# The two arrays of a triangular solver laid transposed in memory, and its GpSimd loops run the other way round

## The chip, the cores and the metric

One core of a Trainium2 chip runs the whole kernel in one launch. The metric is device time in microseconds (us); the kernel before was run three times, and the median is compared. Five engines work side by side: TensorE (PE in the profile; its weight loads stand as PEld), VectorE (DVE), ScalarE (ACT), GpSimd (POOL) and SyncE (SP, which here only issues DMAs). They tell each other of finished work through semaphores.

## The reference

The kernel computes one block of a network on x of shape (2, 4096, 512), all in float32. After a layer norm two branches read the same normed rows and are both added to x:

```python
x = L0_attn_x
xn = _layernorm(x, axis=-1)
x = x + _L0_attn_ref(xn, ...) + _L0_ffn_ref(xn, ...)
```

The attention branch is a gated delta rule: projections to q, k (16 heads of 16) and v (16 heads of 32), a causal convolution of four taps and a SiLU, normalisation of q and k, and then, for every head, a recurrence over the tokens:

```python
S = S * jnp.exp(g_t)[..., None, None]
mem = jnp.einsum('bhk,bhkv->bhv', k_t, S)
delta = (v_t - mem) * b_t[..., None]
S = S + jnp.einsum('bhk,bhv->bhkv', k_t, delta)
o_t = jnp.einsum('bhk,bhkv->bhv', q_t, S)
```

Its output is normed, gated and projected. The feed-forward branch multiplies by weights unpacked from four bits (512 to 2 x 1408, gate and up, then 1408 to 512) and norms the result.

## The kernel before, in words

The tokens are cut into 32 steps. A step takes 128 tokens of both batch rows, so 256 columns. The kernel writes the recurrence in chunks of 32 tokens: inside a chunk the tokens depend on each other through a lower triangular 32x32 matrix A per head, batch row and chunk, and the chunk needs T, the inverse of (1 + A). With 4 chunks on the 128 partitions (32 partitions each), 16 heads and 2 batch rows there are 128 such matrices in a step.

How T is made is where the change lies. The names below are views of one large tile, `arena`:

- `gram_products(b)` (VectorE, lines 991 and 992) multiplies the products of the keys by the decay and writes A into `kbq`, with the tokens of a chunk on the partitions and (batch row, head, column i) along the free side.
- `turn_a` (VectorE, line 971) is one instruction that transposes 32 blocks of 32x32 in each of the four groups of 32 partitions, 1024 elements for each partition. It goes from `kbq` to `la`. After it the 32 pairs (batch row, head) lie on the partitions, and a partition holds one whole triangular matrix in its 1024 elements.
- `solve` (GpSimd, lines 471 to 492) sets `lt` to the unit matrix (lines 478 and 480) and runs 31 steps j of forward substitution. Each step is one multiplication into `work` (line 488) and one subtraction from `lt` (line 492), on r times w elements with w = j + 1 and r = 31 - j.
- `turn_t` (VectorE, line 976) transposes `lt` back into `tT`, which TensorE reads in the next step (`t_times_r`, line 1229).

In the array before, `la` and `lt` are indexed [j, i], row after row of 32 elements. A block turn takes 32 elements with one index fixed. `turn_a` reads `kbq` with the 32 elements of a block 32 elements apart (128 bytes) and writes `la` with its 32 elements as far apart. `turn_t` reads `lt` with a distance of 32 elements and writes `tT` likewise.

The order of the work is written by hand. Each engine has its own function of a step (`dve_step`, `pe_step`, `act_step`, `pool_step`), and each runs its instructions in the order in which they stand there. A step of the loop handles step t's state and output and step n = t + 1's projections and feed-forward. The feed-forward goes in 22 units of 8 matmuls each (lines 1161 and 1162, `xh` and `xl` by `wgu`); ScalarE scales a unit's first part (line 590), VectorE adds the other three (line 884), ScalarE makes the SiLU (line 601), VectorE multiplies (`hidden`, line 896), and `down` (line 1174) multiplies the result by `wdn`. On VectorE the stretch with the first turn runs so:

```python
gram_products(0)
gram_products(1)
turn_a()
hidden(0)
unit(3)
hidden(1)
```

TensorE's `unit(5)` waits for `gram_products` (line 992), and `down(0)`, right after it, for `hidden(0)`. GpSimd, in `pool_step`, does `gated_and_scaled` (lines 510 to 520) for the step before and then `solve`. `turn_t` stands at the end of a step on VectorE, ahead of the two instructions of line 1078 that write the feed-forward result.

Of the kernel before, what the change touches and what calls it, by code (L numbers as in the profile page):

```python
# [28 lines left out]
P = 128  # L29
# [6 lines left out]
CH = 32  # L36
# [51 lines left out]
def bc(ap, n):  # L88
    return ap.unsqueeze(len(ap.shape)).broadcast_to(list(ap.shape) + [n])


def build(nc, A, out):
    NIT = A["x"].shape[1] // P

    with ExitStack() as ctx:

        def sb(name, shape, dt=F32):
            return ctx.enter_context(nc.sbuf_tensor(name, shape, dt))

        def signal(name, per):  # L100
            return Signal(ctx.enter_context(nc.semaphore("s_" + name)), per)
# [40 lines left out]
        arena = sb("arena", [P, 10 * 1024])  # L142
# [13 lines left out]
        work = sb("work", [P, C // 2])  # L156
# [4 lines left out]
        gml = xl[:, :, :].rearrange("p k t -> p (k t)").rearrange("p (b h i) -> p b h i", b=NB, h=H)  # L161
        E = arena[:, 9216:10240].rearrange("p (b h i) -> p b h i", b=NB, h=H)
        D = arena[:, 6144:7168].rearrange("p (b h i) -> p b h i", b=NB, h=H)
        la = arena[:, 0:1024].rearrange("p (j i) -> p j i", j=CH)
        tT = arena[:, 0:1024].rearrange("p (b h i) -> p b h i", b=NB, h=H)
        lt = arena[:, 1024:2048].rearrange("p (j i) -> p j i", j=CH)
        Y = sb("Y", [P, NB, H * DK])
        YT = sb("YT", [P, NB, NHALF, P])
        S = sb("S", [P, NC, NB, NHALF, PV])
# [35 lines left out]
        t_turned = signal("t_turned", 1)  # L205
# [120 lines left out]
        def hold(eng, sem, value):  # L326

            eng.wait_ge(sem, value)
            eng.sem_inc(carrier.sem, 1)
# [141 lines left out]
        def solve(eng, n):  # L471

            if not n.first:
                hold(eng, *t_turned.at(n.before(), 1))
            hold(eng, *qk_done.at(n, NB))
            hold(eng, *kt_done.at(n, NB))
            hold(eng, *rk_done.at(n, NB))
            eng.memset(lt[:, :, :], 0.0).then_inc(lt_eye.sem, 1)
            hold(eng, *lt_eye.at(n, 1))
            eng.memset(arena[:, 1024:2048:CH + 1], 1.0).then_inc(lt_eye.sem, 1)  # L480
            hold(eng, *lt_eye.at(n, 2))
            hold(eng, *a_turned.at(n, 1))
            for j in range(CH - 1):
                w, r = j + 1, CH - 1 - j
                if j:
                    eng.wait_ge(*solve_part.at(n, 2 * j))
                pr = work[:, 0:r * w].rearrange("p (c i) -> p c i", c=w)
                eng.tensor_tensor(pr, la[:, j, j + 1:].unsqueeze(1).broadcast_to([P, w, r]), bc(lt[:, 0:w, j], r),  # L488
                                  ALU.mult).then_inc(solve_part.sem, 1)
                eng.wait_ge(*solve_part.at(n, 2 * j + 1))  # L490
                tail = lt[:, 0:w, j + 1:]
                eng.tensor_tensor(tail, tail, pr, ALU.subtract).then_inc((t_done if j == CH - 2 else solve_part).sem, 1)  # L492

        def layer_norm_scale(eng, m):
# [27 lines left out]
        def pool_step(eng, t, n, more):  # L522
            if n:
                split_x(eng, n)
                expanded_g(eng, t, n)
                masked_g(eng, t, n)
                keys_for_R(eng, t, n)
                if more:
                    layer_norm_scale(eng, n.next())
                rest_of_x(eng, n)  # L530
                next_tile(eng, t, n)
                keys_for_state(eng, t, n)
            if t:
                gated_and_scaled(eng, t)
            if n:
                solve(eng, n)
                feed_forward_scale(eng, n)
# [304 lines left out]
        def dve_step(eng, t, n, more):  # L842
# [123 lines left out]
            def turn_a():  # L966
                if not n:
                    return
                eng.wait_ge(*a_done.at(n, NB))
                eng.wait_ge(*gram_out.at(n, NB))  # L970
                eng.transpose(la.rearrange("p j i -> p i j"),  # L971
                              kbq[:, :, :].rearrange("p b (h i) -> p i (b h)", i=CH)).then_inc(a_turned.sem, 1)

            def turn_t():
                eng.wait_ge(*t_done.at(n, 1))
                eng.transpose(tT.rearrange("p b h i -> p i (b h)"),
                              lt.rearrange("p j i -> p i j")).then_inc(t_turned.sem, 1)

            def gram_products(b):
                if not n:  # L980
# [72 lines left out]
# [5 lines that stand above are left out]
# [7 lines left out]
            for m in range(2, FM):  # L1065
# [5 lines left out]
                if more and m in (7, 9):  # L1071
                    layer_norm_apply(eng, n.next(), (m - 7) // 2)
            turn_t()
            eng.wait_ge(*res_loaded.at(n, 16 * NB))
            for i, b in enumerate((1, 0)):
# [471 lines left out]
def _program(nc, arrays):  # L1547
    A = {k: nc.dram_tensor("in_" + k, v.shape, mybir.dt.from_np(v.dtype), kind="ExternalInput").ap()
         for k, v in arrays.items()}
    out = nc.dram_tensor("out", arrays["x"].shape, F32, kind="ExternalOutput").ap()  # L1550
    build(nc, A, out)
# [12 lines left out]
```

## Time and profile before

| what | us |
| --- | --- |
| median of 3 runs | 3346.0 (3338.62 to 3356.49) |
| the profiled execution, its time | 3346.24 |
| its span in the trace | 3344.4 |
| PE busy | 3162.1 (95%) |
| DVE busy | 2494.0 (75%) |
| POOL busy | 1918.1 (57%) |
| ACT busy | 1667.5 (50%) |
| both block turns together, 64 instructions | 134.5 |
| lines 488 and 492 on POOL, 1984 instructions | 1073.9 |

Busy time is time in which an instruction of the engine was under way; matmuls overlap, so a PE that is busy is not always PE at its peak. The profiled execution's own time is its span and 1.8 us around it. "Granted clock" is the share of TensorE's full clock that the chip granted in a stretch.

### The profile page before, as it was taken

The page shows a single profiled execution, that of the slowest core. Times are in us where ns is not written, and L with a number is a line of the kernel's source. Part 1 is how long each engine was busy: PE and PEld are TensorE (multiplying, and loading weights), DVE is VectorE, ACT ScalarE, POOL GpSimd, SP SyncE. Part 2 cuts the span into 40 slices and gives each one's busy share as a digit, 9 for nine tenths or more (in the row PEclk, how much of TensorE's full clock was granted, in tenths as well). Part 3 has the DMA queues.
Part 4 walks back from the last instruction along what each step waited for, and adds up shares of the span by engine and source line. Part 5 has one row for each costly group of instructions (what it writes and reads, how often), then busy time and mean ns, then how long its engine had stood idle before and what let it go on. Part 6 is the DMA issues. An engine that isn't in the chain of part 4 may idle for free.

```text
span 3344.4 us, 117697 instructions
## 1 busy us (share of the span) xinstructions
PE 3162.1 (95%) x45632; PEld 2269.7 (68%) x45632; DVE 2494.0 (75%) x5472; ACT 1667.5 (50%) x3306; POOL 1918.1 (57%) x2865
## 2 busy tenths in 40 slices
PE   5999999999999999999999999999999999999996
PEld 4676677766667766667766776667677667666664
DVE  6877777777777777777777777777777777777773
ACT  4544555444555544555445555445554455544452
POOL 4566555666555666555665556665556654566643
PEclk8999999999999999999999999999999999999997
DMA  3000000000000000000000000000000000000000
GB/s 117 8 21 21 5 18 21 20 21 15 12 18 21 20 21 8 15 21 21 21 21 5 18 21 20 21 14 9 21 21 20 21 5 18 21 20 21 15 3 21
DMA packets 34157, 64.93 MB, mean 19 GB/s; under 512 B 5216, under 2 KB 7008, under 8 KB 33632
## 3 DMA queue, kind: packets, MB, share of 16 engines
q1 hardware_dynamic: 29664, 52.12, 4.7%
q8 instruction: 383, 6.28, 0.8%
q10 hardware_dynamic: 4096, 6.42, 0.5%
q14 instruction: 14, 0.11, 0.0%
HBM read 41.75 MB, written 16.78 MB: 17 GB/s over the span
## 4 chain that ended last, share of the span: by engine, by line
PE 83%; DVE 12%; issue 4%; ACTq 1%; ACT 0%; POOL 0%; DVEq 0%; POOLq 0%
PE PS L1174 18%; PE PS L1130 13%; PE PS L1161 9%; PE PS L1162 9%; PE PS L1243 7%; PE PS L1383 7%; PE PS L1229 3%; PE PS L1308 3%; DVE arena L884 3%; DVE arena L971 2%; PE PS L1261 2%; PE PS L1279 2%; DVE arena L374 2%; PE PS L1398 2%; DVE arena L991 1%
## 5 line engine op out<-in xcount | busy, mean ns | idle before, releaser
L884 DVE SCALAR_TENSOR_TENSOR arena<-PS,sc,arena 128x256 f32<-128x256 f32 x2112 | 1006.9, 483 | 407.8 <-ACT arena L590 306.2
L1161 PE MATMUL PS<-xh,wgu 128*128 128x256 f32 x2816 | 866.1, 340 | 58.2 <-DVE arena L992 50.7
L590 ACT ACTIVATE arena<-PS,sc 128x256 f32<-128x256 f32 x704 | 333.1, 476 | 891.9 <-PE PS L1162 771.1
L1174 PE MATMUL PS<-wdn,inner 128*128 128x512 f32 x1408 | 693.2, 620 | 32.6 <-DVE inner L896 32.6
L1162 PE MATMUL PS<-xl,wgu 128*128 128x256 f32 x2816 | 700.1, 283 | 0.0
L1161 PEld LDWEIGHTS PS<-xh,wgu 128*128 128x128 f32 x2816 | 534.8, 190 | 164.5 <-issue 87.4
L492 POOL TENSOR_TENSOR arena<-arena,work 128x31 f32<-128x31 f32 (+15 forms) x992 | 554.3, 559 | 77.8
L1162 PEld LDWEIGHTS PS<-xl,wgu 128*128 128x128 f32 x2816 | 533.4, 189 | 83.2 <-issue 83.2
L488 POOL TENSOR_TENSOR work<-arena 128x31 f32<-128x31 f32 (+15 forms) x992 | 519.6, 524 | 98.8 <-POOL arena L480 11.8
L1130 PE MATMUL PS<-xnT,wqkv 128*128 128x256 f32 x2048 | 484.3, 387 | 16.8 <-ACT xnT L560 8.8
L1130 PEld LDWEIGHTS PS<-xnT,wqkv 128*128 128x128 f32 x2048 | 383.1, 192 | 84.0 <-issue 15.3
L1174 PEld LDWEIGHTS PS<-wdn,inner 128*128 128x128 f32 x1408 | 252.1, 196 | 235.2 <-issue 197.3
L868 DVE SCALAR_TENSOR_TENSOR qkv<-inner,cw,qkv 128x256 f32<-128x256 f32 x576 | 291.6, 543 | 54.9 <-ACT qkv L577 48.0
L1243 PE MATMUL PS<-wg,xnT 128*128 128x512 f32 x512 | 264.3, 620 | 1.4 <-issue 1.4
L1383 PE MATMUL PS<-wo,arena 128*128 128x512 f32 x512 | 241.2, 594 | 0.0
L601 ACT ACTIVATE sg<-arena 128x256 f32<-128x256 f32 x352 | 145.4, 413 | 190.9 <-DVE arena L884 190.7
L374 POOL TENSOR_TENSOR R<-arena,ckg 128x256 f32<-128x256 f32 x64 | 57.3, 914 | 304.0 <-DVE ckt L950 304.0
L510 POOL TENSOR_TENSOR arena<-arena 128x512 f32<-128x512 f32 x64 | 80.7, 1283 | 240.8 <-ACT qkv L757 240.8
L609 ACT ACTIVATE ub<-PS 32x512 f32<-32x512 f32 x256 | 136.8, 580 | 160.1 <-PE PS L1261 158.3
L896 DVE TENSOR_TENSOR inner<-arena,sg 128x256 f32<-128x256 f32 x352 | 173.5, 493 | 33.4
L912 DVE SCALAR_TENSOR_TENSOR S<-S,exs,tmp 128x64 f32<-128x64 f32 x512 | 173.2, 379 | 9.1 <-DVE tmp L906 0.2
L515 POOL TENSOR_TENSOR ro<-ro,mhalf 128x32 f32<-128x32 f32 x32 | 174.1, 5439 | 5.9 <-POOL ro L512 5.9
(150 smaller groups left out, 4626.9 us busy)
## 6 DMA issues: line engine op xcount, KB each, us to landing
xt<-in_x SPq DMA_DIRECT2D x64, 256.0 KB, 3.4
obuf<-in_x SPq DMA_DIRECT2D x64, 256.0 KB, 2.8
out<-obuf SPq DMA_DIRECT2D x64, 256.0 KB, 2.0
wqkv<-in_wqkv ACTq DMA_DIRECT2D x1, 2048.0 KB, 13.6
arena<-in_gup ACTq DMA_DIRECT2D x2, 704.0 KB, 6.4
arena<-in_dns SPq DMA_DIRECT2D x1, 1408.0 KB, 12.1
wg<-in_wg ACTq DMA_DIRECT2D x1, 1024.0 KB, 19.9
wo<-in_wo ACTq DMA_DIRECT2D x1, 1024.0 KB, 17.0
```

The lines of the kernel that those rows point to most:

```text
L488: eng.tensor_tensor(pr, la[:, j, j + 1:].unsqueeze(1).broadcast_to([P, w, r]), bc(lt[:, 0:w, j], r), ALU.mult).then_inc(solve_part.sem, 1)
L492: eng.tensor_tensor(tail, tail, pr, ALU.subtract).then_inc((t_done if j == CH - 2 else solve_part).sem, 1)
L515: eng.tensor_tensor(ro[:, :, :], ro[:, :, :], mhalf[:, :, :], ALU.pow).then_inc(ro_done.sem, 1)
L590: eng.activation(fa[:, u % 4, :], PS[:, bank(u, 0), 0:NB * P], ACT.Copy, scale=sc[:, u % 2, KB * m:KB * m + 1]).then_inc(fa_scaled.sem, 1)
L868: eng.scalar_tensor_tensor(out=acc, in0=cin[:, mm, :, k:k + P], scalar=cw[:, mm, k:k + 1], in1=acc, op0=ALU.mult, op1=ALU.add).then_inc((t ...
L884: eng.scalar_tensor_tensor(out=fa[:, u % 4, :], in0=PS[:, bank(u, k // 2), k % 2 * NB * P:][:, 0:NB * P], scalar=sc[:, u % 2, KB * m + k:K ...
L1130: ins = eng.matmul(PS[:, proj_bank(m), 0:NB * P], wqkv[:, kb, m * P:(m + 1) * P], xnT[:, kb, :], start=(kb == 0), stop=(kb == KB - 1))
L1161: eng.matmul(o, w, xh[:, k, :], start=True, stop=False)
L1162: ins = eng.matmul(o, w, xl[:, k, :], start=False, stop=True)
L1174: ins = eng.matmul(PS[:, b, :], inner[:, m, b * P:(b + 1) * P], wdn[:, m, :], start=(m == 0), stop=(m == FM - 1))
L1243: ins = eng.matmul(PS[:, 4 + b, :], xnT[:, kb, b * P:(b + 1) * P], wg[:, kb, :], start=(kb == 0), stop=(kb == KB - 1))
L1383: ins = eng.matmul(PS[:, 6 + b, :], oT[b][:, kb, :], wo[:, kb, :], start=(kb == 0), stop=(kb == KB - 1))
```

## The change

The two arrays are declared with their indices swapped, [i, j] for [j, i], over the same memory. The two turns then name them without a rearrangement, so that `turn_a` writes `la` in one contiguous run (it still reads `kbq` with elements 128 bytes apart) and `turn_t` reads `lt` in one contiguous run (it still writes `tT` with elements 128 bytes apart). In `solve` the loops over a product run the other way round: r rows of w elements, where before they were w rows of r. The column of `la` that a step multiplies by is now read with rows 128 bytes apart, each element repeated w times, as the first operand; before, a row of `lt` was read so as the second operand. The number of instructions, of elements and of waits is the same, and so is their order on each engine. The diagonal of `lt` has the same addresses.

```diff
-        la = arena[:, 0:1024].rearrange("p (j i) -> p j i", j=CH)
+        la = arena[:, 0:1024].rearrange("p (i j) -> p i j", i=CH)
         tT = arena[:, 0:1024].rearrange("p (b h i) -> p b h i", b=NB, h=H)
-        lt = arena[:, 1024:2048].rearrange("p (j i) -> p j i", j=CH)
+        lt = arena[:, 1024:2048].rearrange("p (i j) -> p i j", i=CH)
...
-                pr = work[:, 0:r * w].rearrange("p (c i) -> p c i", c=w)
-                eng.tensor_tensor(pr, la[:, j, j + 1:].unsqueeze(1).broadcast_to([P, w, r]), bc(lt[:, 0:w, j], r),
+                pr = work[:, 0:r * w].rearrange("p (i c) -> p i c", i=r)
+                eng.tensor_tensor(pr, bc(la[:, j + 1:, j], w), lt[:, j, 0:w].unsqueeze(1).broadcast_to([P, r, w]),
                                   ALU.mult).then_inc(solve_part.sem, 1)
                 eng.wait_ge(*solve_part.at(n, 2 * j + 1))
-                tail = lt[:, 0:w, j + 1:]
+                tail = lt[:, j + 1:, 0:w]
...
-                eng.transpose(la.rearrange("p j i -> p i j"),
+                eng.transpose(la,
                               kbq[:, :, :].rearrange("p b (h i) -> p i (b h)", i=CH)).then_inc(a_turned.sem, 1)
...
                 eng.transpose(tT.rearrange("p b h i -> p i (b h)"),
-                              lt.rearrange("p j i -> p i j")).then_inc(t_turned.sem, 1)
+                              lt).then_inc(t_turned.sem, 1)
```

## Rows read from the trace of the kernel before

**Rows 1.** The page, parts 1 and 2: busy time of each engine, granted clock in 40 slices

```profile
PE 3162.1 (95%) x45632; PEld 2269.7 (68%) x45632; DVE 2494.0 (75%) x5472; ACT 1667.5 (50%) x3306; POOL 1918.1 (57%) x2865
...
PEclk8999999999999999999999999999999999999997
```

**Rows 2.** The page, part 4: the chain that ended last, by engine and by line

```profile
PE 83%; DVE 12%; issue 4%; ACTq 1%; ACT 0%; POOL 0%; DVEq 0%; POOLq 0%
PE PS L1174 18%; PE PS L1130 13%; PE PS L1161 9%; PE PS L1162 9%; PE PS L1243 7%; PE PS L1383 7%; PE PS L1229 3%; PE PS L1308 3%; DVE arena L884 3%; DVE arena L971 2%; PE PS L1261 2%; PE PS L1279 2%; DVE arena L374 2%; PE PS L1398 2%; DVE arena L991 1%
```

**Rows 3.** The chain in order of time, 1598 to 1612 us: start, us, what

```profile
1602.11 2.14 DVE arena L971
...
1610.49 0.39 PE PS L1161
```

**Rows 4.** Timeline of VectorE: start, us, instruction, idle before it and its releaser

```profile
1601.51 0.68 DVE L992 TENSOR_TENSOR arena<-PS,arena 128x512 f32<-128x512 f32 x1
...
1604.16 0.37 DVE L896 TENSOR_TENSOR inner<-arena,sg 128x256 f32<-128x256 f32 x1
...
1606.13 1.30 DVE L896 TENSOR_TENSOR inner<-arena,sg 128x256 f32<-128x256 f32 x1
...
1648.55 2.12 DVE L976 STREAM_TRANSPOSE arena<-arena 128x1024 f32<-128x1024 f32 x1 [0.50 <-POOL arena L492]
1652.43 1.41 DVE L1078 SCALAR_TENSOR_TENSOR obuf<-PS,yr,obuf 128x512 f32<-128x512 f32 x2 [1.76 <-POOL yr L504]
...
2216.14 0.43 DVE L896 TENSOR_TENSOR inner<-arena,sg 128x256 f32<-128x256 f32 x1
```

**Rows 5.** Timeline of TensorE, the same step

```profile
1602.24 0.39 PE L1161 MATMUL PS<-xh,wgu 128*128 128x256 f32 x1 [1.59 <-DVE arena L992]
...
1604.58 3.38 PE L1174 MATMUL PS<-wdn,inner 128*128 128x512 f32 x4 [1.13 <-DVE inner L896]
...
1660.66 0.88 PE L1229 MATMUL PS<-R,arena 32*32 32x48 f32 x64
```

**Rows 6.** Groups of VectorE: shapes xcount | busy us, mean ns | idle before

```profile
L971 DVE STREAM_TRANSPOSE arena<-arena 128x1024 f32<-128x1024 f32 x32 | 67.4, 2105 | 0.0
L976 DVE STREAM_TRANSPOSE arena<-arena 128x1024 f32<-128x1024 f32 x32 | 67.1, 2098 | 24.2 <-POOL arena L492 24.2
...
L930 DVE COPY arena<-PS 128x512 f32<-128x512 f32 x64 | 44.0, 687 | 91.5 <-ACT arena L627 88.8 <-PE PS L1186 2.7
...
L906 DVE TENSOR_TENSOR tmp<-PS,bdmask 128x128 f32<-128x128 f32 x256 | 74.2, 290 | 106.1 <-PE PS L1279 101.5
```

**Rows 7.** Busy time from one first turn to the next: length, engines, granted clock, DMA

```profile
180.10:282.70 102.60, 99.33 (x1426) 71.28 (x1426) 77.13 (x171) 51.88 (x103) 59.27 (x90) 0.97 0.06 17
...
484.30:585.20 100.90, 96.92 (x1426) 69.69 (x1426) 76.89 (x171) 51.48 (x103) 59.39 (x90) 1.00 0.05 18
...
2517.50:2619.40 101.90, 97.38 (x1426) 69.68 (x1426) 77.80 (x172) 51.50 (x103) 59.87 (x90) 1.00 0.06 17
...
3028.10:3130.00 101.90, 98.44 (x1426) 70.28 (x1426) 77.86 (x172) 51.49 (x103) 59.91 (x90) 0.98 0.05 17
```

**Rows 8.** Timeline of GpSimd, the same step as in rows 3 to 5

```profile
1606.11 2.23 POOL L520 TENSOR_TENSOR arena<-arena,ro 128x512 f32<-128x512 f32 x2
...
1609.92 0.24 POOL L488 TENSOR_TENSOR work<-arena 128x31 f32<-128x31 f32 x1 [0.38 <-POOL arena L480]
1610.24 0.25 POOL L492 TENSOR_TENSOR arena<-arena,work 128x31 f32<-128x31 f32 x1
...
1647.85 0.32 POOL L488 TENSOR_TENSOR work<-arena 128x31 f32<-128x31 f32 x1
1648.25 0.27 POOL L492 TENSOR_TENSOR arena<-arena,work 128x31 f32<-128x31 f32 x1
```

**Rows 9.** Groups of GpSimd: shapes xcount | busy us, mean ns | idle before

```profile
L488 POOL TENSOR_TENSOR work<-arena 128x31 f32<-128x31 f32 (+15 forms) x992 | 519.6, 524 | 98.8 <-POOL arena L480 11.8 <-DVE arena L971 11.8
...
L374 POOL TENSOR_TENSOR R<-arena,ckg 128x256 f32<-128x256 f32 x64 | 57.3, 914 | 304.0 <-DVE ckt L950 304.0
```

## The prediction

> **What bounds the kernel now.** I read the page first. TensorE is busy 95% of the span and its clock is granted in full in most slices [rows 1]. The chain that ended last goes to TensorE for 83% and to VectorE for 12%, and 2% of it, 67 us, is line 971, the first block turn [rows 2]. That is all that line 971 takes in the whole run (32 x 2.105 us = 67.4 us), so the first turn lies on the path in every step. Line 976, the second turn, takes as long (2.098 us) [rows 6] and is not among the chain's lines.
>
> The chain in order of time shows why, in the step at 1602 us: the turn holds it for 2.14 us and it stays on VectorE until TensorE takes over at 1610.49 [rows 3]. VectorE has no gap around the turn: the product of line 992 ends, the turn runs, `hidden(0)` starts at 1604.16 [rows 4]. TensorE meanwhile waits 1.59 us for line 992 and, after eight matmuls, another 1.13 us for `hidden(0)` [rows 5]. So in this stretch VectorE is the bound, and a nanosecond less in the first turn is a nanosecond less for TensorE.
>
> The second turn ends at 1650.67, and the next instruction of VectorE waits until 1652.43 for `yr`, which hangs on the last `down` and not on the turn [rows 4]. TensorE first uses `tT` at 1660.66 [rows 5]. Up to 1.76 us more or less in `solve` or in the second turn are therefore free.
>
> **The first turn.** It moves 1024 elements for each partition. Both sides step 128 bytes for every element before; after, only the source does. The trace has no turn with a contiguous side, so its price is bounded:
> - From below: contiguous work on VectorE takes 290 ns for 128 columns and 687 ns for 512 [rows 6], so 1.034 ns for a column and 158 ns besides; 1024 columns would take 1.22 us. That is the end if the contiguous side frees the other as well.
> - From above: 2.10 us, the turn as it is [rows 6], if one strided side alone sets the rate. I see no reason for which it would go above: no access gets wider apart, and the pow on GpSimd that runs beside it runs beside it now.
>
> The excess over contiguous work is 2.105 - 1.22 = 0.88 us. [...] I take away somewhat over a quarter of the excess, 0.25 us: 1.85 us. On the path: 32 x 0.25 = 8.0 us.
>
> [...]
>
> **The meeting with GpSimd.** `hidden(1)` starts at 1606.13, within 20 ns of GpSimd's line 520 at 1606.11 [rows 4, 8]. In this step VectorE came second and took 1.30 us where it takes 0.43 in the step at 2216 [rows 4]. It is so in four of the 32 steps, those whose first turn takes 2.14 us or more, and such a step with the full clock is 101.9 us long where one without it is 100.9 [rows 7]. Line 520 hangs on the sums of line 1051 and the pow, both started before the turn, so it stays where it is while `hidden(1)` moves forward by 0.25 us and always comes first. Four times 0.87 us: 3.5 us. GpSimd then waits a little for `hidden(1)`, as it does now in the other 28.
>
> **The clock.** [...] The first of these 29 windows and three others stand in [rows 7]. The 9 with 1.00 have a mean of 101.0 us, the 10 with 0.98 one of 101.6, the 10 with 0.97 one of 102.5: together 10 x 0.6 + 10 x 1.5 = 21 us of falls. The waits are 2.7 us [rows 5] and get 0.25 us shorter, a tenth. If a tenth of what the falls cost goes with them, that is 2 us. Bounds: nothing, and, if the shorter gap saves a third of the falls, 7 us. It can also go the other way (a rival below).
>
> **GpSimd's loops.** 31 multiplications and 31 subtractions for each step, 992 of each in all [rows 9]. The sizes were w rows of r and are r rows of w, with w = j + 1 and r = 31 - j: step j now has the shape that step 30 - j had, so each shape stands as often as before. The first pair, one row of 31, took 0.24 and 0.25 us; the last, 31 rows of one, 0.32 and 0.27 [rows 8], which differ by 0.1 us. What is new is only which operand repeats its elements and which has the rows 128 bytes apart: they change places. I cost it at nothing. Bounds: 0.1 us saved or lost for each multiplication would be 3 us a step; saved, it gives nothing, since the end of `solve` is not waited for; lost, it stays under 1.76 us but for 1.3 us. The far bound is line 374 on GpSimd, also a product with repeated elements, at 0.914 us for 256 elements against a mean of 0.524 for line 488 [rows 9].
>
> **The second turn.** It may get as much shorter, 0.25 us, but VectorE then waits as much longer for `yr`: nothing. The fills of `lt` and its diagonal touch the same addresses with the same steps: nothing. No DMA, no wait and no order changes.
>
> **The sum.** Against the profiled execution (3346.24 us; the span of 3344.4 and 1.8 us around it), 8.0 + 3.5 + 2 = 13.5 us less: 3332.7. That execution stands at the median of the three, 3346.0, so I say 3333 us, 0.4% less. With the clock's bounds and the scatter of the runs, this case's own range is 3325 to 3341.
>
> **The rivals.**
> - The turn does not get shorter, since the strided side alone sets its rate. Then lines 971 and 976 stay at 2.10 us and the time at 3346. [...] Against it: the turn's two sides cost 0.88 us together, and one of them is gone. Chance 0.18.
> - The destination is what costs, or the sides add up: the turn falls by half of its excess or all of it. With half, 0.44 us: 14 us, 3.5 us of meetings and 5 us of clock, 3324. With all, 0.88 us: 28, 3.5 and some 10 us of clock, since the gap shrinks by a third: 3305. For it: how the excess is shared between the sides no row shows. Chance 0.20, more of it at the near end.
> - `solve` gets longer. GpSimd repeats the elements of its first operand now, and if that costs it more than repeating the second did, all 31 multiplications of a step pay. `solve` lasts from 1609.92 to 1648.52; the second turn waits for it, and up to 1.76 us nothing else does. From there on each us is a us in VectorE's line 1078 and the convolution behind it. At 0.13 us for each multiplication (a quarter of 0.524), 4 us a step, 2.3 of them past the slack: 31 x 2.3 = 71 us; less the 13 gained, 3404, slower. At 0.08 us, 2.5 us and 0.7 past it: 3355. For it: GpSimd's 0.914 us row. Against it: rows 128 bytes apart cost it next to nothing in the last pair of `solve`, and the operands are of equal rank. Chance 0.08.
> - The clock falls more often, since a step's length decides where the next waits come to lie, and 9 steps escape now. If all 29 fell at the mean of 1.05 us, that would be 9 more of them, 9 us, which eats most of the gain: 3342. Chance 0.06.
>
> **How the numbers follow.** The forecast has 0.48. A measurement of this kernel can tell some 0.5% (17 us) from no change, so faster means under 3329. Faster: a third of the forecast's case (0.16) and nearly all of the second rival (0.18): 0.34. Slower: most of the solve rival, and a little for the unforeseen: 0.08. The same: the rest, 0.58. The range reaches down to the half-excess case and part of the way to the full one, and up past the unchanged turn with the runs' scatter: 3310 to 3352.
>
> **What would show each step.** In the profile after, line 971 with a mean of 1.8 to 1.9 us (2.1: first rival; under 1.7: second), and line 976 likewise. TensorE's wait for `hidden(0)` near 0.9 us in place of 1.13. No `hidden(1)` of 1.30 us. Lines 488 and 492 at a mean of 524 and 559 ns as before, `solve` of 38.6 us, and VectorE still waiting for `yr` ahead of line 1078. Windows from turn to turn near 100.7 us where the clock is full, with some 18 to 20 of 29 below it. The prediction is wrong if line 488's mean rises by more than 60 ns, if the chain leaves line 971, or if a shorter turn comes with TensorE waiting as long as before.

## The result, and the profile after

Over 20 runs of each, the changed kernel has a median of 3335.84 us (3330.78 to 3340.0) against 3345.01 (3337.95 to 3356.49): a ratio of 0.9972, 95% interval 0.9964 to 0.998, so 9.2 us or 0.27% less. 3333 us was forecast. The profiled execution took 3330.78 us, the shortest of the 20 and 5 us below the median; against the profiled one of before it is 15.5 us shorter, so the two profiles show more than the medians do.

The page after, its chain by line: the first turn, line 971, is still on it with its whole 63 us.

```profile
PE 81%; DVE 13%; issue 4%; ACTq 1%; DVEq 0%; ACT 0%; POOL 0%; POOLq 0%
PE PS L1174 17%; PE PS L1130 13%; PE PS L1161 9%; PE PS L1162 9%; PE PS L1243 7%; PE PS L1383 7%; DVE arena L884 3%; PE PS L1229 3%; PE PS L1308 3%; DVE arena L971 2%; PE PS L1261 2%; PE PS L1279 2%; DVE arena L374 2%; PE PS L1398 2%; DVE arena L991 1%
```

The groups of both engines answer to [rows 6, 9]:

```profile
L971 DVE STREAM_TRANSPOSE arena<-arena 128x1024 f32<-128x1024 f32 x32 | 63.3, 1978 | 0.0
L976 DVE STREAM_TRANSPOSE arena<-arena 128x1024 f32<-128x1024 f32 x32 | 63.1, 1973 | 30.0 <-POOL arena L492 30.0
...
L488 POOL TENSOR_TENSOR work<-arena 128x31 f32<-128x31 f32 (+15 forms) x992 | 518.8, 523 | 98.9 <-DVE arena L971 11.9 <-POOL arena L480 11.8
```

The turns fell from 2.10 to 1.98 and 1.97 us, by 0.127 and 0.125 us. GpSimd's multiplications did not move (523 ns for 524).

The timeline of VectorE, of TensorE and of GpSimd in the step at 1598 us, which answers to [rows 4, 5, 8]:

```profile
1598.55 1.97 DVE L971 STREAM_TRANSPOSE arena<-arena 128x1024 f32<-128x1024 f32 x1
1600.45 0.38 DVE L896 TENSOR_TENSOR inner<-arena,sg 128x256 f32<-128x256 f32 x1
...
1602.44 0.43 DVE L896 TENSOR_TENSOR inner<-arena,sg 128x256 f32<-128x256 f32 x1
...
1647.86 1.41 DVE L1078 SCALAR_TENSOR_TENSOR obuf<-PS,yr,obuf 128x512 f32<-128x512 f32 x2 [1.33 <-POOL yr L504]
```

```profile
1600.89 1.99 PE L1174 MATMUL PS<-wdn,inner 128*128 128x512 f32 x4 [0.98 <-DVE inner L896]
```

```profile
1602.56 2.23 POOL L520 TENSOR_TENSOR arena<-arena,ro 128x512 f32<-128x512 f32 x2
```

`hidden(1)` now starts 0.12 us ahead of GpSimd's line 520, where it was 0.02 us behind it, and takes 0.43 us at most; 1.30 us does not occur. (Line 896 as a whole went from a mean of 493 to 509 ns, all of the rise in its later executions beside the solver.) TensorE waits 0.98 us for `hidden(0)` in place of 1.13 in this step. Over all 32 steps, the mean time from the end of line 992 to the start of `down(0)` went from 2.36 to 2.26 us: of the turn's 0.127 us, 0.10 arrive at TensorE, 3.2 us in the run.

The windows from turn to turn answer to [rows 7]. Three of 30:

```profile
485.90:586.40 100.50, 96.77 (x1426) 69.65 (x1426) 76.81 (x171) 51.49 (x103) 59.07 (x90) 1.00 0.06 18
...
991.80:1093.80 102.00, 98.30 (x1426) 70.31 (x1426) 77.05 (x171) 51.73 (x103) 58.96 (x90) 0.98 0.06 17
...
1699.50:1802.10 102.60, 99.36 (x1426) 71.35 (x1426) 77.43 (x171) 51.83 (x103) 58.98 (x90) 0.97 0.06 17
```

Of the 29 steps between the second and the last first turn but one, the clock falls in 13, where before it fell in 20 and 9 kept it. In a fall the granted clock goes to a lower level, 0.50: in the step at 1602 us of the kernel before it reads 0.50 from 1605 to 1607 us and 0.79 in the microsecond after them. The steps without a fall went from a mean of 101.0 us to one of 100.8; those with one from 102.05 to 101.6. All 29 together take 16.9 us less. Three of the four meetings stood in steps with a fall, so the terms have to be kept apart: the steps with neither are 100.87 us long before (eight) and 100.76 after (16), which makes 3.2 us; the meetings are 3.5 us; the remaining 10 us are fewer and shorter falls.

The falls are of two kinds. A late one begins 1.3 to 2.8 us after the end of line 992, so behind TensorE's second wait, the one for `hidden(0)`: 16 before, 11 after. An early one begins 0.2 to 0.5 us after it, behind the first wait: 4 before, 2 after.

The two profiles exaggerate what the clock contributed. Their granted clocks are 0.975 and 0.982, 0.007 apart, and 0.982 is the highest of the changed kernel's 20 runs. The 49 runs of the kernel before beside the experiments have a mean of 0.9772, the 25 of the changed kernel (the 20 and e12 below) one of 0.9790, only 0.002 apart. Among the runs of either kernel, 0.001 of clock goes with 0.9 to 1.6 us. By that estimate the clock is worth some 2 to 3 us of the medians' 9.2. (On the one chip of e12 the means are 0.9761 for nine runs and 0.9796 for five, which would be 3 to 6 us of the 12.9 there.)

### The profile page after: what moved, and what is told of

Its sections match the earlier page's. It is cut to its first block, busy times and chain, and to the rows that moved or that the text cites. A ratio compares the mean times of both kernels' runs of the same rounds, so it can differ in the third digit from the quotient of the medians.

```text
span 3328.9 us, 117697 instructions
## 1 busy us (share of the span) xinstructions
PE 3141.2 (94%) x45632; PEld 2256.7 (68%) x45632; DVE 2488.1 (75%) x5472; ACT 1665.0 (50%) x3306; POOL 1909.2 (57%) x2865
## 4 chain that ended last, share of the span: by engine, by line
PE 81%; DVE 13%; issue 4%; ACTq 1%; DVEq 0%; ACT 0%; POOL 0%; POOLq 0%
PE PS L1174 17%; PE PS L1130 13%; PE PS L1161 9%; PE PS L1162 9%; PE PS L1243 7%; PE PS L1383 7%; DVE arena L884 3%; PE PS L1229 3%; PE PS L1308 3%; DVE arena L971 2%; PE PS L1261 2%; PE PS L1279 2%; DVE arena L374 2%; PE PS L1398 2%; DVE arena L991 1%
## 5 line engine op out<-in xcount | busy, mean ns | idle before, releaser
L1174 PE MATMUL PS<-wdn,inner 128*128 128x512 f32 x1408 | 677.9, 609 | 30.5 <-DVE inner L896 30.5
## 6 DMA issues: line engine op xcount, KB each, us to landing
wo<-in_wo ACTq DMA_DIRECT2D x1, 1024.0 KB, 16.9
```

What stands on the lines that cost most here:

```text
L1174: ins = eng.matmul(PS[:, b, :], inner[:, m, b * P:(b + 1) * P], wdn[:, m, :], start=(m == 0), stop=(m == FM - 1))
```

## The experiments

Ratios are to the kernel before, run beside each on the same chip, with 95% intervals. Falls are late + early among the 29 steps of one profile each; the same kernel differs by a few of them, and by 0.3 us in its steps without a fall, from one profile to the next (changed and e12; e4 and e10).

| kernel | ratio | line 971, ns | steps with a fall | mean step without one, us |
| --- | --- | --- | --- | --- |
| before | 1 | 2105 | 16 + 4 | 100.98 |
| changed | 0.9972 (0.9964 to 0.998) | 1978 | 11 + 2 | 100.76 |
| e12, changed again | 0.9962 (0.9948 to 0.9975) | 1980 | 10 + 5 | 101.04 |
| e1, la alone | 0.999 (0.9975 to 1.0005) | 1979 | 12 + 3 | 101.08 |
| e2, lt alone | 0.9992 (0.9978 to 1.0006) | 2106 | 14 + 3 | 101.33 |
| e3, flat turns | 0.9861 (0.9837 to 0.9885) | 1232 | 2 + 4 | 100.05 |
| e4, changed, turn late | 0.9913 (0.9891 to 0.9935) | 1956 | 0 + 3 | 100.48 |
| e5, before, turn late | 0.9917 (0.9902 to 0.9932) | 2078 | 0 + 3 | 100.78 |
| e6, changed, turn in the middle | 0.9927 (0.9911 to 0.9942) | 1958 | 0 + 6 | 100.96 |
| e7, before, filler | 1.0025 (1.0015 to 1.0035) | 2128 | 0 + 2 | 102.11 |
| e8, changed, filler | 0.9955 (0.9939 to 0.9971) | 1995 | 0 + 5 | 101.23 |
| e9, flat turns, late | 0.9829 (0.9815 to 0.9842) | 1232 | 0 + 4 | 99.73 |
| e10, as e4 | 0.9908 (0.9892 to 0.9923) | 1953 | 0 + 2 | 100.64 |
| e11, as e5 | 0.9913 (0.9897 to 0.9928) | 2104 | 0 + 8 | 100.61 |

**e1, la alone.** `la` and the first turn as changed, `lt`, the second turn and the direction of the loops as before. Of its edit the line of the product:

```diff
-                eng.tensor_tensor(pr, la[:, j, j + 1:].unsqueeze(1).broadcast_to([P, w, r]), bc(lt[:, 0:w, j], r),
+                eng.tensor_tensor(pr, la[:, j + 1:, j].unsqueeze(1).broadcast_to([P, w, r]), bc(lt[:, 0:w, j], r),
```

> Only la is laid the other way (the first turn writes one contiguous run); lt and the second turn are as before, and the loops of the solver keep their direction, so its first operand now steps 128 bytes for every element. Path theory (the first turn is on the path, the second is not): line 971 at 1.97 us, line 976 at 2.10 us, and all of the change's gain, 3336 us, ratio to before 0.997. Rival A (the gain is the second turn's or the order's): 3345, ratio 1.000. Rival B (a step of 128 bytes costs GpSimd): line 488 rises by more than 10% from 524 ns, solve by over 1.6 us, and the time goes up with it.

Measured: 3341.1 us against 3342.99. That is not told apart from the kernel before, and only just from the changed one (intervals 0.9975 to 1.0005 and 0.9964 to 0.998). The trace shows where the gain may have gone:

```profile
L488 POOL TENSOR_TENSOR work<-arena 128x31 f32<-128x31 f32 (+15 forms) x992 | 612.5, 617 | 97.3 <-POOL arena L480 11.8 <-DVE arena L971 10.2
...
L976 DVE STREAM_TRANSPOSE arena<-arena 128x1024 f32<-128x1024 f32 x32 | 67.0, 2095 | 98.9 <-POOL arena L492 98.9
...
DVE qkv L868 <- ACT qkv L577: 22.3, 31, 1.6
```

The multiplications rose by 93 ns, 2.9 us a step, and VectorE's second turn now waits 3.1 us a step for the solver (0.75 before). So a step of 128 bytes at every element of the first operand costs GpSimd time, as rival B said, but the time did not go up with it. VectorE waits 75 us longer for the solver over the run, and 53 us less for `yr` (1.2 us are left) and 26 us less for ScalarE ahead of line 868 (48.0 us before): slack took all of it. What remains stands earlier in the step. Line 896 meets the longer GpSimd instructions (a mean of 560 ns for 493), and from the first `down` of a step to its last TensorE needs 45.20 us where it needs 44.88 in the kernel before and in the changed one (steps without a fall or a meeting). That is 10 us in 32 steps, about as much as the change gains.

**e2, lt alone.** The second turn and the reversed loops as changed; `la` and the first turn as before.

```diff
-                eng.tensor_tensor(pr, la[:, j, j + 1:].unsqueeze(1).broadcast_to([P, w, r]), bc(lt[:, 0:w, j], r),
+                eng.tensor_tensor(pr, bc(la[:, j, j + 1:], w), lt[:, j, 0:w].unsqueeze(1).broadcast_to([P, r, w]),
...
-                tail = lt[:, 0:w, j + 1:]
+                tail = lt[:, j + 1:, 0:w]
```

> Only lt is laid the other way (the second turn reads one contiguous run), with the solver's loops reversed as in the change; la and the first turn are as before. Path theory: line 971 at 2.10 us, line 976 at 1.97 us, VectorE waits 0.13 us longer for yr, and the time is that of before, 3345, ratio 1.000. Rival A (the second turn or the reversed loops bring the gain): 3336, ratio 0.997.

Measured: 3343.83 against 3342.99. The second turn and the loops bring no gain that these runs can tell (0.9992, 0.9978 to 1.0006); this kernel plus the new `la` is the changed kernel. GpSimd got faster here, line 488 at 506 ns:

```profile
L488 POOL TENSOR_TENSOR work<-arena 128x31 f32<-128x31 f32 (+15 forms) x992 | 501.9, 506 | 100.4 <-DVE arena L971 13.4 <-POOL arena L480 11.8
...
DVE obuf L1078 <- POOL yr L504: 72.5, 32, 3.0
```

The time saved in the solver and the second turn stands in VectorE's wait for `yr`: 72.5 us over the run for 54.1 before. Two things more can be read here. This kernel has the changed kernel's loops without the rows 128 bytes apart, and its multiplications take 506 ns where those take 523: reversing the loops saved 18 ns, and the rows took 17 of them back. And its first turn is as long as before (2106 ns), but seven steps have the meeting of `hidden(1)` with line 520, where the profile of before has four: their number changes from run to run.

**e3, flat turns.** The changed kernel with both turns contiguous on both sides. It leaves out the rearrangement inside a block, so it computes something else.

```diff
-                              kbq[:, :, :].rearrange("p b (h i) -> p i (b h)", i=CH)).then_inc(a_turned.sem, 1)
+                              kbq[:, :, :].rearrange("p b n -> p (b n)").rearrange("p (i j) -> p i j", i=CH)).then_inc(a_turned.sem, 1)
...
-                eng.transpose(tT.rearrange("p b h i -> p i (b h)"),
+                eng.transpose(tT.rearrange("p b h i -> p (b h) i"),
```

> The changed kernel with both turns contiguous on both sides; left out is the rearrangement of the 32 elements of each block, so A and T are not those of the reference. It prices the side that is still strided. If the sides add up, each was worth 0.13 us and both turns go to 1.84 us: ratio 0.994, 3325 us. If one strided side holds most of the rate (a shared pipe), they go to about 1.2 us: 32 x 0.75 = 24 us less than the change and some 6 us of clock, 3306 us, ratio 0.988.

Measured: 3299.95 against 3342.99. Expected was 3306 for the case that one strided side holds most of the rate.

```profile
L976 DVE STREAM_TRANSPOSE arena<-arena 128x1024 f32<-128x1024 f32 x32 | 39.8, 1245 | 49.3 <-POOL arena L492 49.3
L971 DVE STREAM_TRANSPOSE arena<-arena 128x1024 f32<-128x1024 f32 x32 | 39.4, 1232 | 0.0
```

This gives the scale: 1.23 us with no strided side (the prediction's lower bound was 1.22), 1.98 with one, 2.10 with two. The first strided side costs 0.75 us, the second 0.13; whether a shared pipe is behind it, as the expectation has it, no run shows. Against the changed kernel the turn is 0.75 us shorter, `down(0)` starts 0.73 us earlier and a step without a fall is 0.71 us shorter, so the first turn pays nearly in full on the path, and the late falls go from 11 to 2.

**e4, e6, e10: the first turn later on VectorE.** e4 and e10 are one kernel, run in two sessions.

```diff
             gram_products(1)
-            turn_a()
             hidden(0)
...
                 unit(2 * m + 1)
                 hidden(m)
+                if m == 2:
+                    turn_a()
```

> The changed kernel with the first turn moved on VectorE from ahead of hidden(0) to behind hidden(2), some 6 us later, which GpSimd's solver can take since it starts 7.8 us after the turn. Path theory: TensorE's wait of 1.0 us for hidden(0) goes, and the 2 us of the turn leave the stretch in which VectorE is the bound: up to 2 us a step, 60 us, and the falls of the clock with it, 3270 us, ratio 0.978. If VectorE is the bound until long behind hidden(2), only the first part is gained and given back: 3325 to 3336.

> The changed kernel with the late turn once more, beside the three others on one chip: ratio 0.991, as before.

> The changed kernel with the first turn behind hidden(1), ahead of unit(4). The wait of TensorE for hidden(0) goes, but VectorE still does the turn before units 4 and 5, on which TensorE's units 6 and 7 hang: path theory says that the wait is given back there, so only the falls of the clock go, some 8 us: 3328 us, ratio 0.995, with TensorE's waits for line 884 well over the 10 us of the changed kernel. If the place behind hidden(0) is all that matters, it is as fast as the late turn, 0.991.

e4 and e10 have `turn_a()` behind `hidden(2)`, e6 right behind `hidden(1)`. Measured: 3317.85 and 3315.68 us for the late turn, 3323.19 for the middle one. The expected 3270 was a miss. TensorE's wait for `hidden(0)` went, but waits for line 884 took its place, since the units that TensorE waits for next still queue behind the turn on VectorE: 10 us in the changed kernel, 31 in e4, 41 in e6. In the late kernels `hidden(2)` besides takes 0.79 us in every step (0.43 in the changed kernel), since it now starts 0.5 us behind GpSimd's line 520: 0.36 us of VectorE a step.

```profile
PE PS L1162 <- DVE arena L884: 31.1, 65, 0.7
```

A step without a fall is 100.48 and 100.64 us long (e4, e10) and 100.96 (e6), where the changed kernel's two profiles have 100.76 and 101.04: the 2 us did not come. What went in all three are the late falls, 11 and 10 down to none. e6 is the clearest view of their price. Its steps are no shorter than those of the changed kernel and TensorE waits as long in them, only elsewhere; yet its profiled execution is 7.6 and 10.2 us shorter than the changed kernel's two, and by the ratios (0.9927 against 0.9972 and 0.9962) it would be 12 to 15 us, each ratio known to some 5 us. So a late fall costs about 0.7 to 1.4 us, an estimate. e6's six early falls cost nothing: the steps that have one are 100.95 us long, those without any 100.96.

**e5, e11: the late turn on the kernel before**, with the edit of e4.

> The kernel before with its first turn (both sides strided) moved behind hidden(2), as the late turn was tried on the changed kernel, which gave ratio 0.991 and line 971 at 1.96 us. If the layout's gain is only what the turn takes on the path, most of it goes once the turn is late: line 971 at 2.1 us and a ratio of 0.991 to 0.9925, 3313 to 3318 us. If the layout is worth its 9 us wherever the turn stands: 0.994, 3323 us.

> The kernel before with the late turn once more, beside the changed one on the same chip. If the layout is worth nothing once the turn is late, within 0.1% of it; if VectorE is still the bound behind the late turn, the turn's 0.127 us come back as 4 us, 0.12%, which is at the edge of what five rounds can tell.

Measured: 3320.21 and 3317.66 us. On one chip, e11 and e10 are 3317.66 and 3315.68: 2 us apart, where the shorter turn alone would give 4 (and each ratio is known to some 5 us), and where the two kernels in their usual order are 9 to 13 apart. Their steps without a fall are equally long, 100.61 and 100.64. Neither has late falls or a meeting of `hidden(1)` with GpSimd, so this points to the moment at which the turn ends as the source of much of the layout's gain. It does not prove it: line 896 takes a mean of 562 ns in e10 and 487 in e11, 26 us more of VectorE beside the solver, which may hide what the shorter turn gives.

**e9, flat turns and late.**

> The changed kernel with both turns contiguous on both sides (the rearrangement inside a block is left out) and the first turn behind hidden(2). It tells whether a late turn is off the path altogether: if so, 0.75 us less of it gives nothing and the ratio is that of the late turn, 0.991. If VectorE is still the bound right behind it, as TensorE's 31 us of waits for line 884 there say, up to 0.75 us a step is gained again, 24 us, and the ratio is between 0.984 and 0.989.

Measured: 3289.47 us, 26 us less than e10 for a turn 0.72 us shorter (23 us in 32 steps). The late turn is as much on the path as the early one: VectorE is the bound until behind it.

**e7, e8: a filler on TensorE.** One matmul more, before `down(0)`, into a bank that `down(0)` overwrites.

```diff
             unit(5)
+            eng.matmul(PS[:, 1, :], ident[:, :], wdn[:, 0, :], start=True, stop=True, skip_group_check=True)
             down(0)
```

> The kernel before with one matmul of 0.86 us (into a bank that the next one overwrites) added on TensorE in its wait of 1.13 us for hidden(0). The path stays the same. Clock theory: the falls right after the turn, 20 of 29 steps at 1.1 us each, mostly go: 3325 us, ratio 0.994, and steps near 100.9 us. Rival (the falls cost nothing, or come from elsewhere): the clock is as before and the time the same or up to 10 us longer, where the added matmul runs at the lower level and doesn't fit.

> The changed kernel with the same added matmul. With the falls gone in both, what is left between this one and the kernel before with the matmul is the path alone: 32 x 0.127 = 4.1 us for the turn and up to 3.5 us for the four meetings of hidden(1) with GpSimd, so 4 to 8 us below it, some 3319 us, ratio 0.992. If the change had worked by the clock alone, both would be equal.

Measured: 3355.98 us on the kernel before, 3332.01 on the changed one. The first is a miss: the late falls went, from 16 steps to none, and the time rose. VectorE's timeline in e7 shows why:

```profile
1609.39 2.12 DVE L971 STREAM_TRANSPOSE arena<-arena 128x1024 f32<-128x1024 f32 x1
1611.42 0.38 DVE L896 TENSOR_TENSOR inner<-arena,sg 128x256 f32<-128x256 f32 x1
...
1613.41 1.32 DVE L896 TENSOR_TENSOR inner<-arena,sg 128x256 f32<-128x256 f32 x1
```

and in e8:

```profile
1595.83 2.00 DVE L971 STREAM_TRANSPOSE arena<-arena 128x1024 f32<-128x1024 f32 x1
1597.75 0.39 DVE L896 TENSOR_TENSOR inner<-arena,sg 128x256 f32<-128x256 f32 x1
...
1599.74 0.43 DVE L896 TENSOR_TENSOR inner<-arena,sg 128x256 f32<-128x256 f32 x1
```

With the filler the turn takes some 20 ns longer (2128 for 2105 ns, 1995 for 1978). Why is open: TensorE is busy during 93% of it for 61% without the filler, but during 84% in e6, where the turn takes 1958 ns. In the old layout that is enough for `hidden(1)` to come second to GpSimd's line 520 in 21 of 32 steps, where it was 4; in the new layout it happens once. 20 more meetings at 0.87 us are 17 us, the turns differ by 0.133 us x 32 = 4.3 us, and together these are 21 of the 24 us between e7 and e8. From the first `down` of a step to the last, TensorE takes 45.76 us in e7's steps with a meeting and 44.89 in those without, so there a meeting costs its whole 0.87 us. Over the whole step the two differ by 0.46 us only (102.24 and 101.78), since the stretch behind the last `down` is 0.4 us longer in the eight without; why is open.

The step without a fall is besides 0.5 us longer in e8 than in the first profile of the changed kernel, nearly all of it behind the second turn, with no wait that explains it. In e12, the changed kernel once more, the same stretch is 0.3 us longer too. So more than half of it is what one kernel varies by from profile to profile, and the filler does not price the falls by itself.

**e12, the changed kernel again.**

> The changed kernel once more, beside the late turn on one chip: ratio 0.997, and again fewer falls of the clock right behind the turn than the 20 of the kernel before. Were the 13 falls of its first profile chance, this one could have 20.

Measured: 3333.35 us, 15 steps with a fall. The count is again lower than 20, but 15 to 20 is little for one profile each, and e2, with the first turn of before, has 17. The granted clocks of all runs, above, say more.

## Why the prediction was right, and which term was off

- **What bounds the kernel** held: the first turn lies whole on the path (e3, 0.71 us a step for 0.75 of the turn; e9, 26 us for 23), the second is free (e2, a ratio of 0.9992).
- **The turn's price** was mis-sized. 0.25 us was taken off, 0.127 came, and 0.10 of it at TensorE: 3.2 us (4.1 by the turn itself) for the 8.0 predicted. Somewhat over a quarter of the excess over a contiguous turn was the author's estimate, and no run shows it: what the runs showed in its place is 0.127 us of 0.873, 15%. The strided side that remains was held to 72% of the excess; it holds 0.745 us, 85%. The truth lies halfway between the forecast and the first rival, no gain in the turn.
- **The meeting with GpSimd** held: none in 32 steps in place of four, for 3.5 us (e2, with the turn of before, had seven). e7 and e8 show that it hangs on some 20 ns in the turn, and that in a kernel with a slightly longer turn it would happen in two steps of three: the shorter turn keeps clear of a loss of 0.87 us a step.
- **The clock** held as far as the runs tell. 2 us were said, in bounds of 0 to 7. The profiled pair shows 10 us, with 16 late falls becoming 11; but the granted clock of all runs, 0.002 apart and not 0.007, puts it at some 2 to 3 us. What failed is only the view that all falls are of one kind. (The reading of [rows 1] that the clock is granted in full in most slices is wrong besides: a 9 there stands for 90% or more, and 20 of 29 steps have a fall.)
- **GpSimd's loops** held in the outcome, 523 for 524 ns, though not as "nothing": two changes of 17 to 18 ns cancelled (e2). A loop order one step away costs 93 ns (e1). There the rival's price proved wrong: "from there on each us is a us" would make the 1.1 us a step past the slack 35 us, and e1 is no slower than the kernel before. The slack went further, since VectorE's wait ahead of line 868 gave way too.
- **The sum**, 13.5 us, came to 9.2: 3.2 for the turn, 3.5 for the meetings and 2 to 3 for the clock add up to it. The time is close to the forecast, and within the range, because the one term that was wrong by half was small against the whole; the two small terms came out as said.

What stays open: the division of the 9.2 us is an estimate. The number of meetings is known from single profiles, and the stretch behind the last `down` differs by 0.3 us a step between two profiles of the changed kernel, more than the turn's 0.10. Open are also that stretch in e7 and e8, and how much the late turn's gain from the layout is hidden by line 896.

The version that beats both is the late turn (e4, e10): 3315.68 us, against 3333.35 for the changed kernel on the same chip, 0.5% less, and 0.9908 of the kernel before; on the layout of before (e11) it is as good within the noise. The flat turns (e9) show a further 26 us, for whoever finds a layout of `kbq` and `tT` that needs no stride.

## What to carry to other kernels

Making one of the turn's two strided sides contiguous bought 15% of what both would have: price both ends first, by a version that is contiguous throughout, even one that computes something else. Look at what starts right when the shortened instruction ends, since an instruction on another engine within 20 ns of the next one can be worth more than the shortening (here 3.5 us of meetings for the turn's 3.2). A profile is one run: compare its granted clock with that of the other runs before a difference is put down to the clock. And when a bound engine is relieved of an instruction in front of a waiting TensorE, ask whether the same instruction only waits further down the same queue (here TensorE's waits for line 884 went from 10 us to 31 and 41).

## What the runs showed of the hardware

- A block turn of 1024 float32 columns takes 1.232 us with both sides contiguous (e3, e9; 1.245 at the end of the step), 1.978 with the source stepping 128 bytes (changed), 1.966 to 1.987 with the destination doing so (changed, e12, e2), 2.105 with both (before). The spread goes with it: 1229 to 1246 ns for the contiguous ones, 2057 to 2150 for the one with two.
- The turn with one strided side takes 1.953 to 1.958 us behind `hidden(1)` or `hidden(2)`, and 1.995 with the filler on TensorE (1.978 without). No single neighbour explains all of these.
- A VectorE product of 256 columns that starts 9 to 98 ns behind GpSimd's line 520 took 1.24 to 1.32 us in place of 0.43 (before, e2, e7, e8); in the late kernels, where it starts 0.5 us behind it, it took 0.78 to 0.81 us.
- GpSimd's product pays for a first operand that steps 128 bytes at every element: 617 ns (e1) for 524 (before), at a mean of 176 elements some 0.5 ns an element. The same step between rows of repeated elements costs 17 ns (523 for the 506 of e2).
- TensorE's clock went to its lower level, 0.50, behind a wait of 1.6 us and a second of 1.1 us in 16 of 29 steps (before) and 14 (e2), with a second of 1.0 us in 10 to 12 (changed, e12, e1), of 0.2 to 0.3 us (e3) in 2, and with the second wait gone (e4, e6, e9) in none. Behind the first wait alone it fell in 2 to 8 steps of every kernel; in e6 that cost no time, while in the kernel before its four steps are 101.8 us long for 101.0. In e6 the same waiting in another place came without late falls and 8 to 10 us shorter, so here a second wait soon after a first cost more than its length.
